# One decoder layer on one core: the last fp32 32-row-tile maxima replaced by 64-row bf16 stacks, with a new instruction order

## The reference, cut to what matters

```python
# self-attention (the other parts: cross-attention, then experts)
q = (x @ Wq + bq).reshape(Bx, Tx, N, D).transpose(0, 2, 1, 3)     # N = 16 heads, D = 8
k = (x @ Wk + bk).reshape(Bx, Tx, N, D).transpose(0, 2, 1, 3)
v = (x @ Wv + bv).reshape(Bx, Tx, N, D).transpose(0, 2, 1, 3)
scores = jnp.einsum('bntd,bnsd->bnts', q, k) / jnp.sqrt(jnp.float32(D))
scores = jnp.where(causal[None, None], scores, -jnp.inf)
attn = jax.nn.softmax(scores, axis=-1)
out = jnp.einsum('bnts,bnsd->bntd', attn, v)
...
x = x + _L0_attn_ref(_layernorm(x, axis=-1), ...)
x = x + _L0_xattn_ref(_layernorm(x, axis=-1), ctx_1024, ctx_1024, mask, ...)
x = x + _L0_ffn_ref(_layernorm(x, axis=-1), ...)
```

## Time and profile before

| | |
|---|---|
| median of 3 runs | 330.28 us (328.94 to 337.8) |
| the profiled execution, device time | 332.62 us |
| its span, first to last instruction | 330.9 us |
| instructions | 6805 |
| busy share: TensorE (PE), DVE, ACT, POOL | 88%, 74%, 55%, 40% |
| mean granted TensorE clock | 0.950 of full |

### The profile page before, as it was taken

How to read it: one execution, slowest core, us unless ns; L and a number is a source line. 1 busy time by engine, 2 the same in 40 slices (tenths; PEclk the granted TensorE clock), 3 DMA queues, 4 the chain that set the end, 5 groups by cost and what they waited for, 6 DMA issues and landing times. The chain is left out here.

```text
span 330.9 us, 6805 instructions
## 1 busy us (share of the span) xinstructions
PE 292.6 (88%) x2512; PEld 140.3 (42%) x2512; DVE 245.3 (74%) x655; ACT 182.3 (55%) x348; POOL 132.6 (40%) x201
## 2 busy tenths in 40 slices
PE   6998999999999989999779998989978786997891
PEld 2584435454544443545433353443423343233440
DVE  6599998899889998889997343774943379344486
ACT  4732686878597288695564556567427701651000
POOL 5183362427545072053210059535781210248033
PEclk9999999999999999999955999979998999999698
DMA  3853350003402042030000000103000120000001
GB/s 86 232 128 98 85 146 4 0 4 82 115 23 76 4 124 71 5 97 4 2 4 0 6 0 0 34 2 95 2 4 32 34 67 4 1 0 24 11 0 32
DMA packets 19921, 14.36 MB, mean 43 GB/s; under 512 B 2704, under 2 KB 19888, under 8 KB 19888
## 3 DMA queue, kind: packets, MB, share of 16 engines
q1 hardware_dynamic: 19584, 13.66, 15.5%
q10 hardware_dynamic: 304, 0.26, 0.2%
HBM read 2.58 MB, written 1.05 MB: 11 GB/s over the span
## 5 line engine op out<-in xcount | busy, mean ns | idle before, releaser
L813 ACT ACTIVATE probs<-banks 128x512 f32<-128x512 f32 x160 | 86.6, 609 | 28.2 <-PE banks L1206 25.3
L913 DVE TENSOR_REDUCE peaks<-banks 128x1 f32<-128x384 f32 (+3 forms) x154 | 87.8, 633 | 7.1 <-PE banks L1163 6.8
L702 POOL TENSOR_SCALAR_AFFINE_SELECT probs<-probs 128x512 f32<-128x512 f32 (+1 forms) x80 | 43.6, 549 | 72.3 <-ACT probs L813 72.3
L713 POOL TENSOR_TENSOR yw<-yw 128x512 f32<-128x512 f32 (+2 forms) x42 | 34.3, 818 | 36.5 <-issue 16.2
L1222 PE MATMUL banks<-probs,v_s 128*9 128x256 f32 (+3 forms) x512 | 42.9, 434 | 0.2
L819 ACT ACTIVATE xprobs<-banks 77x512 f32<-77x512 f32 x64 | 33.3, 594 | 15.2 <-PE banks L1231 13.7
L1206 PE MATMUL banks<-q_stack,k_stack 64*128 64x128 bf16 (+3 forms) x256 | 41.0, 307 | 0.5 <-DVE xpeaks L926 0.3
L1163 PE MATMUL banks<-k_stack,q_stack 62*128 62x256 bf16 (+3 forms) x224 | 41.3, 307 | 0.0
L1159 PE MATMUL banks<-causal_slot,pick_slot 64*128 64x128 bf16 (+2 forms) x308 | 38.0, 249 | 1.3 <-DVE peaks L913 0.5
L1269 PE MATMUL banks<-expert_w_s,normed_t 128*128 128x512 f32 x64 | 34.9, 648 | 1.7 <-DVE yw L1017 1.2
L1017 DVE TENSOR_TENSOR yw<-banks,g_comb 128x512 f32<-128x512 f32 x32 | 21.7, 689 | 19.1 <-PE banks L1269 18.7
(11 more groups left out here) (159 smaller groups left out, 431.0 us busy)
## 6 DMA issues: line engine op xcount, KB each, us to landing
q_stack<-parts_q SPq DMA_DIRECT2D x24, 128.0 KB, 2.5
k_stack<-parts_k SPq DMA_DIRECT2D x24, 128.0 KB, 2.5
xq_stack<-parts_x SPq DMA_DIRECT2D x24, 128.0 KB, 2.4
state<-in_x SPq DMA_DIRECT2D x4, 256.0 KB, 4.8
out<-state SPq DMA_DIRECT2D x4, 256.0 KB, 2.3
expert_w_s<-in_expert_w SPq DMA_DIRECT2D x1, 512.0 KB, 4.9
xk_stack<-parts_x SPq DMA_DIRECT2D x6, 77.0 KB
q_stack<-peaks_t ACTq DMA_DIRECT2D x16, 8.0 KB
```

The lines of the kernel that those rows point to most:

```text
L702: gp.affine_select(out=v, in_=v, compare_op=ALU.is_ge, fill=0.0, base=0, pattern=pattern, channel_multiplier=-1).then_inc(causal_done, 1)
L713: link(gp.tensor_tensor(y[:, 0:n], y[:, 0:n], y[:, n:2 * n], ALU.add))
L813: ac.activation(probs[:, grp % 2, u, :], bank_of(step), ACT.Exp, scale=SCALE).then_inc(taken_of(step), 1)
L913: ve.tensor_reduce(peaks[:, f, t, heads[0]:heads[0] + n, s], bank_of(step)[:, 0:n * width].rearrange("p (h k) -> p h k", h=n), X_AXIS, ALU ...
```

## The change

The set of halves computed by 32-row tiles becomes empty. With it `project_kt`, `project_qt` (their ACT work too) and the 24 `tile_peak` steps are no longer in the plan, and 22 `peak` steps of half 0 of batch 0 take their place, which need both stacks. Besides, `FILL` goes from 1.0 to 0.7, three bounds in `AHEAD` go down by one, and the tie-breaking order of the eight chains is another. What only served the tiles and stands outside the plan stays: the loads of `wk_ts`, `wq_ts`, `bk_ts`, `bq_ts`, ACT's copy to `causal_rows`, DVE's `pick` and `q_bias`.

```diff
--- before.py
+++ after.py
@@ -33,7 +33,7 @@
 TILE = 32
-TILED_PEAKS = ((0, 0),)
+TILED_PEAKS = ()
@@ -81,12 +81,12 @@
 LATENCY, HOP, SWITCH, ISSUE, LAND = 0.22, 0.05, 0, 0.645, 1.9
-WINDOW, BUSY, COLD, FILLER, FILL = 3.413, 1.5, 0.5, 0.216, 1.0
+WINDOW, BUSY, COLD, FILLER, FILL = 3.413, 1.5, 0.5, 0.216, 0.7
 DRAIN, FORCE, CHILL = 0.09, 0, 0
-BIAS = (0.0, 0.0, 0.0, 0.0, 0.0, 0.0, 0.0, 0.0)
-AHEAD = {'peak': 4, 'tile_peak': 5, 'xpeak': 4, 'scores': 3, 'xscores': 4, 'expert': 2}
-
-ORDER = ('cross', 'context', 'scale', 'peaks', 'experts', 'prepare', 'scores', 'attend')
+BIAS = (0.0, 0.0, 0, 0.0, 0.0, 0.0, 0.0, 0.0)
+AHEAD = {'peak': 4, 'tile_peak': 5, 'xpeak': 3, 'scores': 2, 'xscores': 4, 'expert': 1}
+
+ORDER = ('cross', 'prepare', 'scale', 'context', 'experts', 'scores', 'peaks', 'attend')
```

## The result

| | before | after |
|---|---|---|
| median of 4 runs beside each other | 330.01 us | 356.7 us (352.74 to 358.05) |
| the profiled execution, device time | 332.62 us | 357.89 us |
| its span | 330.9 us | 356.1 us |
| mean granted TensorE clock | 0.950 | 0.926 |

The ratio is 1.078, with an interval of 1.065 to 1.0911: the changed kernel is about 26 us slower. The forecast was 334 us, at most 343.

A forecast was written before the change was run, and what follows sets the result against it. DVE's first-pass reductions bound it to about 160 us, then a chain of dependent steps. Late start +12.5 - 5.0 - 0.5 = +7.0, less 3.1 won back, order 0: 330.3 + 3.9 = 334.2 us, range 322 to 343.

The forecast's parts named there:

- The start: Batch 0: DVE's first stack maxima 12.5 us late, less 5.0 moved work and 0.5 fewer reductions: maxima end +7.0 us.
- Half of 6.2 us is won back: Until 157 us: late DVE finds peak banks full, regaining 3.1 us of its waits for TensorE; +3.9 us remains.
- ACT can catch that up: Second pass's first score product comes 8 to 9 us late; ACT, with 29 us to spare, can make it up.
- I carry it to the end unchanged: From 157 us to the end: the remaining +3.9 us stays, as batch 3's maxima still feed its scores.
- The new order at 0, with 8 us both ways: Whole plan: new tie order counted as 0, bounded by gaining or losing one half-clock stretch, up to 8 us.
- rival 3: New order wins more than the start loses, at 160 to 190 us and later: 326 or 321 us; chance 0.23.
- Thinner fillers save nothing themselves: Fillers stand in foreseen gaps, so fewer of them gain no time and only risk the clock.
- Does the hole cool TensorE?: Between 12 and 26 us: a colder clock costs a few tenths on the first product; counted as nothing.
- Rival 2: Full +7.0 start plus up to 8 from clock stretch or starved peaks, second pass and tail: 337–345 us; chance 0.27.
- Rival 4: The start costs nothing, its 7 us lateness being taken up by slack before the end: 329 to 332 us; chance 0.05.

The follow-up runs named there:

- same_order: Kernel before without tiles, its order of all other steps written out, with context, second norm and 22 stack maxima put before the first split; 342.77 us, 1.0376.
- order_only: Changed kernel with the tiles put back, so only the new ORDER, AHEAD and FILL against the kernel before; 353.67 us, 1.0727.
- before_lategate: Kernel before, planned anew with batch 3's query projection held until the third group of values of batch 0's cross-attention; 340.79 us, from one execution.
- fill_only: Kernel before with its own order written out and only FILL lowered to 0.7; 331.97 us, 1.0041.
- after_fill2: Changed kernel with its own order written out, FILL 1.0 and a plan constant that puts in more fillers; 354.22 us, 1.0737.
- after_peaks_up: Changed kernel with one swap in ORDER, peaks in front of scores instead of behind, planned anew; 371.76 us, 1.1262.
- tiled_ORDER: Kernel before, tiles kept, with only the changed kernel's ORDER; 359.44 us, 1.0897.
- tiled_AHEAD: Kernel before, tiles kept, with only the changed kernel's lower AHEAD bounds; 361.42 us, 1.0958.

## Why the prediction was wrong, by its own steps

**The start: right.** DVE's first stack maximum at 27.39 us (26.7 forecast), SP's key stack issued by 19.79 + 3.80 = 23.59 us (23.6), batch 0's maxima done at 57.59 us (56; 56.28 in same_order), the first L1206 at 47.86 us (about 45, given as 44 to 46: 2 to 3 us more). Reading the queue's rows one after another from the last weight load gave DVE's start to within a microsecond; the end of batch 0's maxima is 8.8 us late, where the sum had 7.0.

**"Half of 6.2 us is won back": wrong, 3 us off.** With the order held the lateness was +7.4 us at 56 and at 87 us and +8.3 at 139 us, and the waits for TensorE's peak products grew from 6.2 to 7.6 us. So a DVE that comes late does not find full banks. Why is only argued: the banks bound how far TensorE goes ahead, and TensorE's own steps wait for DVE's splits and come late with them. I had noted that "some move along"; all of them did. DVE's idle time from 57 to 161 us was forecast at 5 to 6 us, and was 9.1 in same_order and 20.1 in after, by the windows (7.3 in before).

**"ACT can catch that up": it didn't.** The four mixing copies of batch 0 (L826) show it. In same_order each of them is 7.4 to 7.5 us later than in before, from the first (56.17 against 48.73 us) to the last (81.57 against 74.12); in after the lag grows from 9.1 to 13.0 us (87.13 against 74.12). Time to spare on ACT did not bring the second pass forward.

**"I carry it to the end unchanged": too little.** In same_order the lateness is +8.3 us at 158 us (the first half of batch 3), where the forecast had +3.9; +6.0 at batch 3's last maxima had become +9.2 at the end of the profiled execution, and 12 us by the ratio. The start's term should have been +9 to +12 and not +3.9; 342 us would have been the forecast for the tiles alone.

**"The new order at 0, with 8 us both ways": the step that failed most.** It cost 24 us with the tiles in place (order_only), and 14 us on top of same_order (356.7 against 342.77). I took its bound from the half-clock stretch of the earlier trace rows, because that was the row that showed waste. That stretch did go (clock 1.00 from 160 to 190 us in after), as rival 3 had it, but others came (0.71 from 265 to 300 us), and no gain shows. The waste came where the earlier trace rows shows none: in the dense part, in which before's order keeps DVE at 93 of 100 us. The better bound lay in the same rows: where an order keeps the bound engine idle for 8.6 of 108.1 us, a new one can win 8.6 us at most there and lose much more. TensorE's time there went to the second pass: 12.0 us less for the peaks of the first pass from 80 to 180 us in order_only, and 67 maxima taken instead of 88. I had the mechanism in one sentence (`scores` before `peaks` starves DVE's main work) and put it at "a little", bounded by waits of the old order. In order_only DVE idles 20.1 us from 80 to 180 us, 12.9 more than before, for its share products (L954, 7.4 us), for peaks (6.9 us) and for the values (L905, 3.5 us); in after mostly for peaks. Waits of DVE from 80 to 176 us, after:

```profile
DVE peaks L913 <- PE banks L1163: 13.0, 9, 3.8
DVE share L954 <- PE banks L1059: 2.1, 1, 2.1
```

and before:

```profile
DVE peaks L913 <- PE banks L1163: 4.1, 7, 0.9
```

**The sum as it came out** (after against before, from the account): 5.0 us idle in the start, 1.7 up to 80 us, 10.7 in the middle, 1.1 behind it, and 6.6 us of longer DVE work: 25.1 us, and the spans differ by 25.2. In before_lategate idle time of the middle partly came back behind 180 us; here none did.

**"Thinner fillers save nothing themselves": right;** they cost 0.4% (fill_only, 1.0041).

**"Does the hole cool TensorE?": it does, and no price of it shows.** The granted clock from 14.2 to 33.1 us is 0.82 where it was 1.00. TensorE had stood idle for 4.36 us before 18.26 us, waiting for the expert weights; the clock is 0.70 from 14.2 to 20 us, 0.75 to 26.7 us and 1.00 from there to 33.1 us, so the first maxima did not run cold. DVE's start came 0.7 us behind the forecast that counted nothing for the clock; no run prices it by itself. The Trainium skill, "TensorE: Matmul & The Clock Gate", section "Why this matters for your kernels", warns of such gaps; the trace agrees that the clock fell, and shows it back at full before the first maxima.

**The rivals.** Rival 2 (the full start, and starved peaks) named the right mechanism in "starved peaks", and its sign by which to know it, DVE's idle time before 157 us staying at 8 us or more, came true with 20.6 us from 48.9 to 157 us. Its place was wrong, as it put the damage in the second pass of batches 2 and 3 and in the tail, and its price of up to 8 us came from the clock. Rival 3's sign was a clock of 1.00 from 160 to 190 us with an earlier end; the clock came and the earlier end didn't. Rival 4 is out by same_order, in which a start 7.4 us late costs 12 us.

**What stays open.** No single swap explains the 10.7 us in the middle. The slots explain 2.4 us of after at most, the clock hardly any (after_fill2), and the rank of `peaks` can't be priced by after_peaks_up, because there the slots take its place; nor does one of the edits by itself do it (tiled_ORDER and tiled_AHEAD are each slower than both together). What the traces show is that TensorE does more of the second pass and less of the first in that stretch, that batch 1's values are done 26 us late all the same, and that DVE then has 107.6 us to do behind 180 us instead of 83.4, of which 12.8 us are one half of the maxima of batch 3. Which swap in the list starts it, I can't say.

## What to carry to other kernels

A planner's parameters are a matched set and belong to one list of steps: price a step with the order held by hand, or between two plans that were both selected, and not by switching it off under the old parameters (36 us here, against 12 by each of those two ways). Bound what a new order may cost by the density of the bound engine, not by the visible waste: with DVE 93% busy over 100 us, the five other orders tried here with the tiles in place and no search cost 10 to 32 us, and the one that was searched for cost nothing. Set the span down as busy plus idle time of that engine by stretch, before looking for a cause; it shows in one table which theories are worth a run.

## What the runs showed of the hardware

DVE's small instructions get longer under another order. The 48 that write the normalised state (first before, then after; mean ns behind the comma):

```profile
L889 DVE TENSOR_SCALAR normed<-state,moments,rstd 128x128 f32<-128x128 f32 x48 | 15.5, 384 | 3.2 <-POOL rstd L661 3.0
```

```profile
L889 DVE TENSOR_SCALAR normed<-state,moments,rstd 128x128 f32<-128x128 f32 x48 | 17.6, 427 | 5.7 <-POOL rstd L661 5.6
```

The reductions out of PSUM did not change (633 ns on the mean in before, 632 in after). What stands beside the slower ones can be read from the timelines. Four of them at 266 us of after, and GpSimd at the same time:

```profile
266.37 3.16 DVE L889 TENSOR_SCALAR normed<-state,moments,rstd 128x128 f32<-128x128 f32 x4 [0.53 <-POOL rstd L661]
```

```profile
266.31 2.61 POOL L713 TENSOR_TENSOR yw<-yw 128x512 f32<-128x512 f32 x3
```

Four such instructions with nothing of GpSimd beside them took 1.12 us (from 6.79 us of the same trace). Of the 48 in after, 17 ran with no GpSimd instruction at the same time and took 338 ns on the mean; the other 31 took 476 ns, and all 11 that took over 400 ns are among them. In before it is 339 ns (22) against 422 ns (26), and the 8 over 400 ns all ran beside GpSimd. Taken over all of DVE's instructions, what they took beyond the lower quartile of their kind (where that is over 50 ns) adds up to 7.7 us in before and in same_order and to 11.3 us in after, and every one of these instructions ran beside GpSimd. Over all, DVE was busy 251.9 us in after and 247.1 in same_order, with 645 instructions in both; so most of that difference is time beside GpSimd. The times of GpSimd in a profile are rough, and which of the two waited can't be read there. The Trainium skill, "SBUF — State Buffer", section "SBUF: two separate sides", says that some DVE instructions and GpSimd's share a pair of ports, and that the second to start waits for the whole of the first; the traces agree with that, and they show no ports.
